# A graph network's relation products: a sixth relation by Strassen's scheme, and key comparisons five to a unit

## What is computed

```python
# x: (625, 1024), weight: (8, 1024, 1024), 20625 edges (src, dst, type)
out = x @ root + bias
for r in range(8):
    mask = (edge_type == r).astype(x.dtype)
    sums = segment_sum(x[src] * mask[:, None], dst, 625)
    cnt = segment_sum(mask, dst, 625)
    out = out + (sums / maximum(cnt, 1)[:, None]) @ weight[r]
z = concatenate([out, x]) @ w_gate + b_gate
h = tanh(out) * z + x * (1 - z)
```

## Time and profile before

| | us |
|---|---|
| median of 3 runs | 1109.83 |
| lowest, highest | 1107.57, 1111.14 |
| the profiled execution | 1113.76 |
| its span, first to last instruction | 1112.0 |
| matmuls | 5385 |
| TensorE busy | 1066.2 |
| VectorE busy | 793.0 |
| ScalarE busy | 413.9 |
| GpSimd busy | 417.4 |

### The profile page before, as it was taken

How to read it: one execution, slowest core, us unless ns; L and a number is a source line. 1 busy time by engine, 2 the same in 40 slices (tenths; PEclk the granted TensorE clock), 3 DMA queues, 4 the chain that set the end, 5 groups by cost and what they waited for, 6 DMA issues and landing times.

```text
span 1112.0 us, 14475 instructions
## 1 busy us (share of the span) xinstructions
PE 1066.2 (96%) x5385; PEld 891.4 (80%) x5385; DVE 793.0 (71%) x1591; ACT 413.9 (37%) x647; POOL 417.4 (38%) x272
## 2 busy tenths in 40 slices
PE   6998999999999999999999998999979999999995
PEld 5776887777787777889999998887756878888774
DVE  7567888889989897317667776495479648876647
ACT  3331333434434343122332323361443415256652
POOL 6023488788788888212442330000010000410016
PEclk9999999999999999999999999999989999989998
DMA  9999978788977776799999742523242201588757
GB/s 322 400 331 383 327 181 145 193 218 208 223 193 147 196 140 161 169 244 219 271 261 252 170 126 99 208 83 126 60 80 89 76 2 59 223 281 277 235 180 258
DMA packets 94475, 217.34 MB, mean 195 GB/s; under 512 B 29978, under 2 KB 46173, under 8 KB 85947
## 3 DMA queue, kind: packets, MB, share of 16 engines
q1 hardware_dynamic: 39488, 137.19, 36.5%
q0 software_dynamic: 37504, 48.18, 21.8%
q10 hardware_dynamic: 17406, 30.97, 10.1%
HBM read 149.59 MB, written 66.71 MB: 195 GB/s over the span
## 4 chain that ended last, share of the span: by engine, by line
PE 78%; DVE 10%; DMA 6%; ACT 3%; issue 1%; ACTq 1%; POOLq 0%; SPq 0%; DVEq 0%
PE ps L583 65%; PE ps L891 3%; PE ps L928 3%; DVE rl L414 3%; DVE EQ L1578 3%; DMA stage<-in_w_e 2%; PE ps L855 2%; DMA stage<-in_w_rel 2%; DMA KR<-key_scratch 2%; PE ps L573 1%; ACT rh L405 1%; DVE V L1498 1%; ACT He L1106 1%; PE ps L939 1%; PE ps L906 1%
## 5 line engine op out<-in xcount | busy, mean ns | idle before, releaser
L2219 POOL DMA_INDIRECT adj_scratch<-cnt,idx x164 | 288.9, 1762 | 133.8 <-issue 43.6
L414 DVE TENSOR_TENSOR rl<-stage,rh 128x512 fp32r<-128x512 f32 (+1 forms) x264 | 213.4, 837 | 152.3 <-ACT rh L405 148.7
L405 ACT CAST rh<-stage 128x512 fp32r<-128x512 f32 (+1 forms) x264 | 180.4, 716 | 364.9 <-PE ps L583 242.8
L583 PE MATMUL ps<-rh,xTh 128*125 128x512 f32 x600 | 239.0, 398 | 5.7 <-ACT He L1106 4.6
L583 PE MATMUL ps<-rl,xTh 128*125 128x512 f32 x600 | 237.5, 396 | 0.0
L583 PE MATMUL ps<-rh,xTl 128*125 128x512 f32 x600 | 237.4, 396 | 0.0
L583 PE MATMUL ps<-rh,Ar 125*125 125x342 f32 x600 | 190.8, 323 | 5.4 <-issue 4.0
L583 PE MATMUL ps<-rl,Ar 125*125 125x342 f32 x600 | 190.3, 322 | 0.0
L583 PEld LDWEIGHTS ps<-rh,xTh 128*125 128x125 f32 x600 | 112.0, 187 | 35.9 <-ACT He L1106 7.2
L583 PEld LDWEIGHTS ps<-rh,xTl 128*125 128x125 f32 x600 | 112.1, 187 | 28.4
L583 PEld LDWEIGHTS ps<-rl,xTh 128*125 128x125 f32 x600 | 112.0, 187 | 27.4
(11 more groups left out here) (295 smaller groups left out, 1615.1 us busy)
## 6 DMA issues: line engine op xcount, KB each, us to landing
stage<-in_w_rel SPq DMA_DIRECT2D x22, 1024.0 KB, 6.4
stage<-h_scratch SPq DMA_DIRECT2D x24, 855.0 KB, 7.3
stage<-in_w_e SPq DMA_DIRECT2D x16, 1024.0 KB, 6.6
adj_scratch<-Z POOLq DMA_DIRECT2D x16, 767.0 KB, 20.1
adj_scratch<-Z SPq DMA_DIRECT2D x16, 767.0 KB, 16.1
h_scratch<-He ACTq DMA_DIRECT2D x40, 257.0 KB, 9.1
h_scratch<-He ACTq DMA_DIRECT2D x40, 256.0 KB, 4.7
KR<-key_scratch ACTq DMA_DIRECT2D x37, 256.0 KB, 6.5
```

What stands on the lines that cost most here:

```text
L405: e.copy(h, s).then_inc(*a_hi.up(*[("hi", t) for t in step(i)]))
L414: e.tensor_tensor(l, s, h.bitcast(F32), ALU.subtract).then_inc(*v_lo.up(*[("lo", t) for t in step(i)]))
L583: ins = e.matmul(ps[0:P, b, 0:width], a, m, start=first and n == 0, stop=last and n == len(parts) - 1, skip_group_check=again)
L2219: e.indirect_dma_start(accd[to], bass.IndirectOffsetOnAxis(ap=idx[:, n:n + 1], axis=0), cnt[:, n:n + 1], None, compute_op=ALU.add).then_in ...
```

## The change

Unit 3 (relation 2) becomes a sum unit, so that six relations of eight go by the scheme. Its windows go elsewhere: the first half of unit 2 has three windows instead of six, and each sum unit five instead of four. The two pieces of S are made in the two halves of unit 2 instead of the second half of unit 2 and the first of unit 3. Positions n count from 0, so (1, 0) is the first half of unit 2.

```diff
-WINDOWS = {(0, 1): (0, 2, 4, 6), (1, 0): (0, 1, 2, 4, 5, 6), (1, 1): (0, 2, 4), (2, 0): (2, 4, 6), (2, 1): (0, 2, 4, 6),
+WINDOWS = {(0, 1): (0, 2, 4, 6), (1, 0): (0, 2, 4), (1, 1): (0, 2, 4),
            (8, 0): (), (8, 1): ()}
...
-FAST = (4, 5, 6, 7, 8)
+FAST = (3, 4, 5, 6, 7, 8)
 KINDS = ("b11", "t2", "t3", "t1", "t4", "b21", "b22")
 FL = 4 * len(KINDS)
-KEYS_IN_FAST = {u: (3, 10, 17, 24) for u in FAST}
-S_IN = ((1, 1), (2, 0))
+KEYS_IN_FAST = {u: (2, 8, 13, 18, 24) for u in FAST}
+S_IN = ((1, 0), (1, 1))
```

## The result

The changed kernel takes 1119.55 us (median of 6 runs, 1116.58 to 1122.31) against 1109.88 for the kernel before (6 runs): the ratio is 1.0085, 95% interval 1.0065 to 1.0106. It is 9.7 us **slower**; 1106.0 was predicted, with a range of 1099 to 1114. The profiled execution took 1120.88 us, its span is 1119.1, 7.1 more than that of before. Later experiments ran beside other sets of runs of the kernel before, with medians of 1109.3 to 1112.7; across sets I compare ratios, and 0.001 is 1.1 us. One execution of e5, of 1118.67 us, counts as slow and is in its median and range but not in its ratio.

A forecast was written before the change was run, and what follows sets the result against it. TensorE's stream was taken as the bound from 170 to 500 us. The terms -5.4 - 5.9 + 3.6 + 0.35 + 1.6 + 2 gave -3.8 us, from a median of 1109.83 to 1106.0 us, range 1099 to 1114.

The forecast's parts named there:

- unit 3 becomes a sum unit: TensorE's time for unit 3 falls from 55.5 to 50.1 us: -5.4 us.
- Five windows: The fifth window of each sum unit, 3.1 us, fits in VectorE's 4.3 us of idle time: 0.
- S before the first sum unit: In unit 2's second half VectorE's list takes 31.6 us, so S is ready at 142.6 and TensorE waits.
- The first bank: Before the first sum unit TensorE waits for ScalarE's copies to free PSUM banks: +3.6 us, and +0.35 for the second.
- V2: In the first sum unit VectorE writes V2 at 157.6, TensorE wants it at 156.0: +1.6 us.
- Loads: b12 of unit 3 lands after the first sum wants it, holding VectorE: +2 us, bounds 0 to 5.
- the hole goes: With three windows, not six, in unit 2's first half, TensorE's hole near 105 us and its low clock vanish: -5.9 us.
- nothing behind the spreads changes: From the start of the spreads on, nothing changes except by being earlier.
- POOL and the adjacency: Before the spreads, POOL's adds end 0 to 5 us later, but some 7.5 us of cover are left: 0.
- POOL sets the start of the spreads: Rival, chance 0.08: slower POOL adds delay the spreads, gain 0 to 3, 1107 to 1110 us.
- the boundary is cheap: Rival, chance 0.20: VectorE or ScalarE reach S earlier before the first sum unit, 1098.5 to 1102 us.
- VectorE the bound in the sum units: Rival, chance 0.20: five windows bind VectorE at V2 and V3, up to 3.1 us a unit, 1121.4 us.

The follow-up runs named there:

- e5: e3 with ScalarE's last cast of a piece of S behind the half's five copies out of PSUM: 1110.11 us, ratio 0.9982.
- e3: The changed kernel with twelve of SP's sixteen writes of zeros moved behind the loads of unit 3: 1107.18 us, ratio 0.9975.
- e8: e3 with one window less in the second half of unit 2 and one in the first half of unit 0: 1103.63 us, ratio 0.9946.
- e1: The kernel before with only the windows moved, five in each of its five sum units: 1106.97 us, ratio 0.9977.
- e7: The kernel before with twelve of the sixteen writes of zeros moved behind the first two loads of unit 3: 1117.56 us, ratio 1.0079.
- e12: The kernel before with the writes of zeros four by four behind loads 6, 9, 10 and 11: 1105.89 us, ratio 0.9944.
- e16: The kernel before with only ScalarE's second adjacency copy moved behind the casts of the first two h tiles: ratio 0.9994.
- e17: e12 with ScalarE's second adjacency copy moved behind the casts of the first two h tiles: 1102.70 us, ratio 0.9937.
- e6: e3 with the round of PSUM banks set to bank 7 at the start of the spreads: 1108.07 us, ratio 0.9996.
- e10: e8 with ScalarE's last cast of a piece of S behind the half's five copies out of PSUM: 1112.14 us, ratio 0.9998.

## Why the prediction was wrong

**Right.** The step *unit 3 becomes a sum unit* (-5.4): 24 matmuls are gone at 0.231 us each, and the sum units behind it stay 50.1 us apart. *Five windows*: 0. *S before the first sum unit*: VectorE's list was put at 31.6 us from its first split to S. Changed: 113.11 to the cast at 153.01, 39.9, less 7.75 of waits for loads, is 32.1; in e3 108.23 to 140.35 is 32.1 as well. *The first bank*, +3.95: 4.1 in e3. *V2*, +1.6: 1.5 in e8, where the first bank's wait was only 0.9; none in e3, behind the low clock; in the changed kernel 0.4 over a matmul, since t2 was late itself and then ran at the low clock. GpSimd's adds did not slow down (median 1651 ns, before 1704), so the lengthening of up to 5 us that I had allowed for did not come, although single adds do take longer beside VectorE's sums: in the trace of before 1.54 us beside nothing on VectorE, and 1.97 in the median beside a sum. Such adds were 32 before and 36 after, of 164. (The add at 271.81 of the earlier trace rows, which I took as one beside an idle VectorE, had a split beside it for a part.)

**Wrong, first: *Loads*, +2 us, bounds 0 to 5.** This is the step that failed. I priced b12 alone and by the landing times of stage loads. b11 (3.3), b12 (2.2) and b22 (5.6) were all late, 11.1 us of VectorE's time in a list without slack. b22 is an operand of the sums, so the new sum unit needs it a whole half ahead of its matmuls; it stood behind 7.3 writes of zeros and a load on SP's queue, and took 27 us. A median over loads that nobody hurried says little of a load at the end of a full queue. Putting the loads first (e3) took 12 us off. In that half the term measured 7.75 us (2.2 and 5.6) where the sum had 2; b11's 3.3 came in the half before, where the sum had no term for it.

**Wrong, second: *the hole goes*, -5.9.** Moved alone (e1) the windows do take it away, but 4.2 us come back at the next boundary. In the changed kernel S and the late b11 meet in that very half: VectorE is 3.4 us late at 104.78, and the hole stays at 3.4 + 1.7. I had written "a little late ... net 0", and compared with an equal half inside unit 3, where the DMA engines are no longer full (DMA share 0.79 in the earlier trace rows, 1.05 from 104 to 131 us in the changed kernel). That the hole would have gone with the loads in time is shown by e3.

The two are 5.1 (the hole that stayed) and 12.1 less 7.55 (the second hole with its clock and V2, against 3.95 + 1.6 + 2), 9.7 in all. From the forecast of -3.8, less 0.7 for a gap at 76.6 that is gone, that makes +5.2, the +5.1 read off above but for rounding.

**Wrong, third: *nothing behind the spreads changes*.** From the spreads to the end the span grew by 2.2 us. Some 1.3 lies near 690. There TensorE has a wait before that the profile puts down to issue (4.00), and after the change two waits for VectorE (0.76 and 4.39). VectorE has a wait of that kind there in both (3.34 before, 3.41 after), so that alone is not the difference. After, then before:

```profile
690.46 0.39 PE L583 MATMUL ps<-rh,Ar 125*125 125x342 f32 x1 [0.76 <-DVE U L1673]
...
698.27 1.10 PE L573 MATMUL ps<-ident,U 125*128 125x125 f32 x4 [4.39 <-DVE U L1673]
```
```profile
689.44 0.39 PE L583 MATMUL ps<-rh,Ar 125*125 125x342 f32 x1 [4.00 <-issue]
```

In the traces of the experiments, all thirteen with six sum units have that pair of waits, and all five with five sum units (e1, e7, e12, e16, e17) the one wait of 3.3 to 4.0. So it belongs to the change; its cause is open, and e6 shows that it isn't the order of the banks.

Of the medians' 9.7 us, 4.9 lie before the spreads and 2.2 behind them in the profiles; 2.6 are how the two profiled executions stand to their medians (3.9 and 1.3 above).

**Wrong without effect on the forecast: *POOL and the adjacency*, 7.5 us of cover.** I took the first adjacency copy as the reader. The second copy, ScalarE's cast behind it and GpSimd's sum beside VectorE's split come before the second h tile, and TensorE waited 1.44 us there already. Had my gain come, this place could have taken it, as in e10; e3 and e8, whose spreads start at 492.87 and 488.50, show that it need not. The rival *POOL sets the start of the spreads* (0.08) did not come true in the changed kernel; it had the engine of e10's loss, but not the instruction. Of the other rivals, *the boundary is cheap* is refuted by the hole of 10.5 us, *VectorE the bound in the sum units* by the distances.

## What to carry to other kernels

A step that pulls data forward pulls its loads forward too: list every load the new order needs, with its issue time, what stands ahead of it on its queue, and the time its first reader wants it, and look for slack before pricing it. A removed hole was a lead for all that follows; find the next late item behind it. And where a gain must pass a hand-over near its end (here adjacency to spreads), read every wait at that place in the trace of before, even one of 1 us.

## What was not expected of the hardware

- A load of 1024 KB issued on SP's queue with 7.3 writes of 767 KB and a load still ahead of it landed after 27.2 us, 19.6 of them before its first packet. In e7, behind twelve writes issued one after another, a cast waited 14.35 us for its load.
- VectorE's split of 125x1710 takes 1.94 us by itself and up to 8.58 when GpSimd's sum of 128x3125 runs beside it: it ends 1.8 us behind the sum, whether it began at the sum's start or near its end (2.39 in most of those).
- ScalarE's five copies out of PSUM with a store each hold it for 5.2 us (1.04 apart). Where VectorE had nothing else left to do, it idled for 5.0 to 5.8 us at the boundary of a half (5.74 at 113.11 and 4.98 at 159.31 in the changed kernel).
